# Two mixture-of-experts stages of a Trainium2 kernel: rows gathered two pairs further ahead, into ten buffers in place of eight

## The reference

```python
E, K, F = (64, 8, 192)
C = 128
logits = x @ router_w.T
topk_w, topk_ids = jax.lax.top_k(softmax(logits), K)
...
xb = x_buf[:E * C].reshape(E, C, -1)          # the first C tokens of each expert
g = jnp.einsum('ecd,edf->ecf', xb, w_gate)
u = jnp.einsum('ecd,edf->ecf', xb, w_up)
h = silu(g) * u
y = jnp.einsum('ecf,efd->ecd', h, w_down)
contrib = y[safe] * (flat_w * valid)[:, None]
routed = segment_sum(contrib, tok, num_segments=T)   # added into the tokens' rows
```

## Time and profile before

| | us |
|---|---|
| median of three runs | 2587.45 |
| lowest and highest | 2583.96, 2590.21 |
| the profiled execution | 2582.3 |
| its span | 2580.6 |
| PE busy in the span | 2395.2 (93%) |
| DVE, ACT, POOL busy | 1651.4, 1366.6, 1150.1 |
| clock granted to PE, mean | 0.958 |

### The profile page before, as it was taken

The page is one execution under the profiler, slowest core; times in us unless marked ns, Lnnn a source line. Parts: engine busy times, 40 slices in busy tenths (PEclk is TensorE's granted clock), DMA queues, the critical chain, the costliest instruction groups (busy, mean ns, idle before and its releaser), DMA issues. The chain is left out here.

```text
span 2580.6 us, 48369 instructions
## 1 busy us (share of the span) xinstructions
PE 2395.2 (93%) x14822; PEld 1295.1 (50%) x14822; DVE 1651.4 (64%) x3745; ACT 1366.6 (53%) x2766; POOL 1150.1 (45%) x1497
## 2 busy tenths in 40 slices
PE   7997999999999999979998996899999969997997
PEld 4664233333333333356556664566666646555765
DVE  6777888888888888446552322688888746553321
ACT  4666677767766776646522322455555427632322
POOL 6998111111111011123326775677777724324776
PEclk9998799999999999989999998999999989998999
DMA  5655423232333232136767874011111026585886
GB/s 172 204 194 173 124 84 100 86 101 84 97 87 99 86 96 64 37 123 201 244 212 195 231 196 75 16 37 38 38 38 34 20 75 204 194 279 159 228 206 110
DMA packets 286870, 325.20 MB, mean 126 GB/s; under 512 B 30496, under 2 KB 272368, under 8 KB 286704
## 3 DMA queue, kind: packets, MB, share of 16 engines
q1 hardware_dynamic: 252928, 274.22, 33.9%
q0 software_dynamic: 29184, 46.43, 9.0%
q10 hardware_dynamic: 4592, 2.47, 0.4%
HBM read 217.29 MB, written 105.19 MB: 125 GB/s over the span
## 5 line engine op out<-in xcount | busy, mean ns | idle before, releaser
L716 DVE TENSOR_REDUCE a_row_max<-a_ps_m 128x2 f32<-128x1024 f32 x512 | 607.4, 1219 | 84.6 <-PE a_ps_m L619 79.6
L776 ACT ACTIVATE a_probs<-a_ps_s 128x512 f32<-128x512 f32 x1024 | 536.8, 602 | 206.9 <-PE a_ps_s L647 206.6
L662 PE MATMUL a_ps_o<-a_probs,a_va 128*32 128x512 f32 x2048 | 274.1, 608 | 0.8 <-ACT a_o_sb L785 0.8
L1738 POOL TENSOR_TENSOR b_spread<-b_decay,held_own_sb 128x512 f32<-128x512 f32 x256 | 269.0, 1082 | 8.2 <-DVE b_weight L1799 8.2
L1799 DVE TENSOR_TENSOR b_weight<-b_ps_s,b_spread 128x512 f32<-128x512 f32 x256 | 163.7, 681 | 17.6 <-PE b_ps_s L1939 17.6
L647 PE MATMUL a_ps_s<-first_qs,first_ks 98*128 98x512 bf16 (+1 forms) x512 | 161.0, 396 | 3.1 <-DMA first_qs<-a_m_parts 3.1
L647 PE MATMUL a_ps_s<-second 98*128 98x512 bf16 (+1 forms) x512 | 157.0, 387 | 4.4 <-DMA second<-a_m_parts 2.3
L556 POOL CAST a_high<-a_row_max 128x32 bf16<-128x32 f32 x32 | 6.5, 204 | 316.2 <-DVE a_row_max L716 316.2
L597 POOL DMA_DIRECT2D x<-a_xo x32 | 24.2, 755 | 275.3 <-DVE a_xo L750 272.9
L1558 DVE SCALAR_TENSOR_TENSOR m2e_h<-m2e_act_g,m2e_xg,m2e_ps_h 128x192 f32<-128x192 f32 x64 | 26.5, 414 | 150.7 <-ACT m2e_act_g L1487 132.9
L315 PE MATMUL a_ps_qk<-a_w_qk,a_xnT 128*128 128x512 f32 x256 | 122.6, 602 | 0.0
(11 more groups left out here) (381 smaller groups left out, 5389.6 us busy)
## 6 DMA issues: line engine op xcount, KB each, us to landing
parts<-second SPq DMA_DIRECT2D x16, 1536.0 KB, 6.2
second<-parts SPq DMA_DIRECT2D x384, 64.0 KB
rows<-m_early SPq DMA_DIRECT2D x32, 640.0 KB
m_early<-x SPq DMA_DIRECT2D x31, 512.0 KB
first_qs<-parts SPq DMA_DIRECT2D x192, 64.0 KB, 2.7
first_ks<-parts SPq DMA_DIRECT2D x192, 64.0 KB, 2.3
m_own<-in_L_ffn_w_gate_dram SPq DMA_DIRECT2D x24, 384.0 KB, 6.8
m_own<-in_L_ffn_w_up_dram SPq DMA_DIRECT2D x24, 384.0 KB, 7.0
```

The source lines that it names most:

```text
L662: last = nc.tensor.matmul(ps_o[VW * j:VW * (j + 1), :], va[n.u][:, t, (h0 + j) * VW:(h0 + j + 1) * VW], probs[:, group % 2, j, t, :], star ...
L716: nc.vector.tensor_reduce(row_max[:, n.k // 4 % 2, t, :, n.p % 4], m_bank(name, step)[:], AX.X, ALU.max).then_inc(m_drained, 1)
L776: nc.scalar.activation(probs[:, group % 2, j, t, :], s_bank(name, step)[:], ACT.Exp, scale=DK ** -0.5).then_inc(s_drained, 1)
L1738: nc.gpsimd.tensor_tensor(spread[:, n % 2, heads].rearrange("p h t c -> p (h t) c"), decay[:, n % 3, heads].rearrange("p h (t o) -> p (h t ...
```

## The change

`xg` gets ten buffers, and every lag but that of the gathers (which is 0) grows by two. All functions of PE, DVE and ACT have a lag, so their order among themselves stays; on POOL the gathers, whose lag stays 0, move two pairs ahead of the scatters. The gather of pair i now waits for pair i - 10. The two further buffers take 5 KB in each partition.

```diff
@@ moe_experts @@
-    WB, XB, YB, DB = len(const["w_buffers"]), 8, 4, 6
+    WB, XB, YB, DB = len(const["w_buffers"]), 10, 4, 6
     slots, slots_f = const["slots"], const["slots_f"]
 
-    L_SAME, L_TURN, L_GU, L_TURN_H, L_DOWN, L_SCATTER = 2, 3, 4, 5, 6, 7
+    L_SAME, L_TURN, L_GU, L_TURN_H, L_DOWN, L_SCATTER = 4, 5, 6, 7, 8, 9
```

## The result

The changed kernel took 2590.9 us (median of 20 runs, 2583.69 to 2597.63), the kernel before, measured beside it, 2583.82 (20 runs, 2576.25 to 2592.73). The ratio is 1.0026 with a 95% interval of 1.0015 to 1.0038: slower, by some 7 us. I had forecast 7 us in the other direction, down from 2587.45, the median of the first three runs, which lay 3.6 us above that of the twenty. The profiled execution took 2593.0 us, with a span of 2591.3.

A forecast was written before the change was run, and what follows sets the result against it. POOL's chain of scatters and landings was taken as the bound. Start and middle zero, end 3.7 + 3.4 = 7.1 us (0.27%), gave 2580.3 us from the median 2587.45; range for 8 in 10: 2571 to 2590.

The forecast's parts named there:

- What bounds the kernel: Expert stages: POOL's stream of gathers, scatters and waits for landings is the longer chain; PE merely follows from pair 15.
- The gain for PE: Middle of the second stage: PE moves ahead once, by 3 to 6 us, then four y buffers hold it.
- Start, "so they cost nothing": Each expert stage's start: four more gathers fit in the 9.33 us idle before the first scatter; cost zero.
- the 5.0 I gave for missing cover: Start of each stage: four extra gathers at 1.25 us would cost 5.0 us without the idle time.
- The rule of the Trainium skill: Start: a ring is consumed in order, so the scatter stands behind all gathers; the sum was held to stay.
- Middle, zero: Middle steps: PE's waits for rows go, but POOL does not wait for PE, so the gain is zero.
- collisions: Slower rival: weight loads fall on the next scatter and loaded steps grow; +7 us (2594) at 0.5 a step; chance 0.13.
- End, 7.1 us: Each stage's end: two steps from pair 23 to 25 lose their gathers; 3.7 us in the second stage, 3.4 first.
- The fit of the Trainium skill: Rival: landing never waited for, so gathers' issue is all saved at the end; 10.3 us, 2577; 3 in 100.
- a first scatter later than 26.7 us after the first gather: Stage start in the changed profile: one of three signs that would show the forecast wrong.
- the bound of PE: Rival: PE's lost time returns, 16.1 us second stage, perhaps 9 first; 25 us, 2562; 0.14 with the page's fit.

The follow-up runs named there:

- f3: Kernel before plus four full-size gathers into a spare tile ahead of the first scatter, second chip; 2565.76 us, kernel before 2572.72 (one run each).
- e4: Changed kernel gone half way: nine buffers, lags one more than before, sixteen gathers ahead; 2589.26 us, 1.0019 of the kernel before.
- k1: Kernel before plus four full gathers into a spare tile ahead of the first scatter, fourth chip; 2595.34 us, kernel before 2584.10.
- k2: Kernel before plus four gathers of 128 rows of 64 bytes in that place, fourth chip; 2594.97 us, kernel before 2584.10.
- k3: Kernel before plus four additions on POOL, no DMA, ahead of the first scatter, fourth chip; 2579.92 us, kernel before 2584.10.
- e1: Kernel before with ten buffers for gathered rows but the old lags and POOL order; 2582.38 us, 1.0005 of the kernel before.
- e2: Changed kernel with POOL pausing after eight gathers until the first two pairs have their h; 2585.06 us, 1.0011 of the kernel before.
- e3: Kernel before with the same pause of POOL after eight gathers; 2583.24 us, 1.0000 of the kernel before.
- h2: Changed kernel, unaltered, profiled again on a third chip, without the stall; 2570.90 us, 0.9991 of the kernel before.
- h1: Kernel before, unaltered, profiled again on the third chip; 2583.74 us in one run, 2572.73 over 25 runs there.
- h: Set of four on a third chip: both kernels, before plus four gathers, changed with a later pause; ratios to before 0.9991 to 1.0009.
- e: Set of four on one chip: buffers only, a pause in either kernel, half the change; ratios to the kernel before 1.0000 to 1.0019.
- k: Set of three on a fourth chip: kernel before plus four full gathers, small gathers or additions; 2595.34, 2594.97, 2579.92 us, before 2584.10.
- f: Set of three on a second chip: kernel before plus four additions, small gathers or full gathers; 2571.74, 2571.68, 2565.76 us, before 2572.72.

## Why the prediction was wrong

**What bounds the kernel: right.** POOL's chain of scatters and landings bounds the middle. PE's waits for rows went (but for the 3.8 us of the first two pairs), and the loaded step is 7.05 and 7.01 us where it was 6.98 and 7.24. Over all profiles it is 6.84 (f3, second stage) to 7.24 whatever the kernel. The gain for PE was stopped by the four y buffers, as stated.

**Start, "so they cost nothing": this step failed.** It took the idle 9.33 us before the first scatter as room of fixed length, and asked only whether POOL's work fits in. Its other end was not fixed. It was set by y, y by a Silu that stands ahead of it on ACT, and that Silu, in these profiles, by the end of POOL's gathers: in all seven profiles with the stall, in both stages, the second Silu of pair 1 starts 1.6 to 3.2 us after the last gather of the run has ended. So the added gathers pushed both ends. The price was 6.6 and 6.4 us where I had 0, more even than the 5.0 I gave for missing cover. Half a mechanism is known: the experiments show that ACT's stall is prolonged by further indirect DMAs in an unbroken run (e4, k1), as much by small as by full rows (k2), not by other work of POOL (k3), not by the buffers (e1), and that it does not appear when POOL pauses after eight gathers (e2, e3). Why it stops ACT at all is not shown. That the clock adds its part is read from the profile alone.

The rule of the Trainium skill (DMA: Bandwidth & Descriptors, "Queues, rings and completion order"), a ring consumed in order, was not what decided. In the changed kernel the scatter is issued late, since it waits for y. And in h2, where it is issued 0.30 us behind the eighteenth gather (2356.01), the next one of its half, which waits for its landing, starts at 2362.42: it landed within 6.4 us, behind all those gathers. The trace does not speak against the rule; it shows no scatter held up by it.

**Middle, zero: right** within what the profiles can tell: 23 steps gained 5.3 us in the second stage and lost 1.6 in the first, and the runs of one and the same order differ by as much (e1 against before: 7.13 to 6.98, 7.02 to 7.24). No mean of a stage rose beyond that, so no collisions show.

**End, 7.1 us: right, slightly too large.** The two gatherless steps gave 12.74 - 9.28 = 3.5 us (forecast 3.7) and 12.77 - 9.21 = 3.6 (3.4). Over the whole end, to pair 31, it is 2.6 and 3.8 us, as six steps behind them took 28.0 us in place of 27.2 in the second stage. In h2 against h1 it is 3.4 in the first and 2.8 in the second. Landing without load was 3.75 us again. The fit of the Trainium skill (DMA: Bandwidth & Descriptors, "Anatomy of one DMA"), by estimate 2.3 us for such a scatter and 10.3 us of gain, does not hold for it: the measured landing and the 7.0 us that the four gatherless steps gave decide.

**Sum.** +6.6 + 6.4 - 2.6 - 3.8 = +6.6 us by the profile's heads and ends, and 1.0026 of 2583.8 us is +6.7 (3.9 to 9.8). The agreement is better than the scatter of single profiles lets one expect, and in part luck: with the middle of the same two profiles (+1.6 and -5.3) the sum would be +2.9. On the chip of h, without the stall, the same sum of heads and ends is 2.3 + 1.6 - 3.4 - 2.8 = -2.3 us, measured 0.9991, which can't be told from none. That heads count in time is borne out between the sets of runs: the changed kernel's two heads are 21.1 us shorter in h and its median 20.0 us lower, those of the kernel before 12.1 us shorter and its median 11.1 us lower. Two chips can differ in other things, so this is no proof.

**The rivals.** None had this cause. The slower rival was collisions of weights and scatters, and its sign came out by another road. The prediction did name the sign of its own failure, "a first scatter later than 26.7 us after the first gather". Two slips in it decide nothing: the program has seven blocks and not five stages, and by the ratio of excesses that it names (0.61 to 0.87) the bound of PE would give back 11 us in the first stage, not 9.

**Still open:** what ACT waits for in the stall, and why two of the four chips of the experiments showed it in no profile. Whether it goes with the chip or with something else that differed between the sets of runs was not tested apart. Also open is why e3's shorter heads don't show in its time, and no version here beat both kernels.

## What to carry to other kernels

Idle time in front of an instruction is cover only if what ends it does not depend on the engine that is to fill it: follow the releaser back to its own last stall, above all where the profile names "issue", "remote" or a long-ended DMA, before booking work at zero. A run of indirect DMAs ahead of a pipeline's first result is a place to look: a pause in it shortened the head here (24.2 us in place of 26.8), though no gain in time was measured. The same change cost 0.26% in one set of runs and nothing that could be measured on another chip; where 0.3% is at stake, repeat both timing and profile on another one.

## What the runs showed of the hardware

- In the stages' first 25 us ACT waited before two Silus for 5.5 to 6.4 us together with 14 gathers in a row, 8.6 with 16 and 9.6 to 11.1 with 18, where it waited 1.7 us without the stall. Nothing visible held it, and POOL issued indirect DMAs every 1.25 us. The DMA engines were not full: from 2367 to 2376.5 in the changed kernel 1.16 MB went, with only the gathers' queue in the row (packets, MB, share of 16 engines). No packet of the queues that bring instructions lies there.

```profile
q0 software_dynamic: 349, 1.16, 41.1%
```

- The stall was in the profiles of three sets of runs (before and after; e, but for its two kernels with a pause; k), growing with the run in each, and absent from two (f; h), of which h had the same two kernels. The kernel before took 2581.51 us on the chip of e and 2572.73 on that of h.
- Four matmuls with 384 columns took 2.93 us right behind a wait of 9.44 us and the product for y (granted clock 0.50), and 1.70 us behind a wait of 4.64 us (0.90). Behind waits of 9.96 and 10.27 us (k1, k2) they took 2.44 and 2.30 us, so the length of the wait alone doesn't set it.
